# Pre-norm graph network, two layers, one Trainium2 core: second norm and adjacency products per row block, degree columns moved in front of the softmax, waits for one block instead of all

## The reference

```python
h = relu(layernorm(x))
feat = concat([h[src], h[dst]], axis=1)            # per edge; three kinds of edges, each with its W, b
e_f = relu(feat @ W_kind + b_kind)
logit = e_f @ W_a + b_a
alpha = segment_softmax(logit, dst)
z = segment_sum(alpha[:, None] * h[src], dst)
x = x + relu(concat([h, z]) @ W_hn_or_on + b)      # nodes 0..127: hn, the others: on
h = relu(layernorm(x))
# second layer: adjacency with self loops, deg = row sums, norm = deg^-0.5[row] * deg^-0.5[col]
x = x + segment_sum(norm[:, None] * (h @ W.T + b)[col], row)
```

## Time and profile before

| | us |
|---|---|
| median of 3 runs | 651.68 |
| runs | 649.97, 651.68, 654.79 |
| profiled execution, whole | 648.16 |
| its span in the profile | 646.0 |
| TensorE busy | 556.7 |
| VectorE busy | 453.9 |
| ScalarE busy | 306.2 |

### The profile page before, as it was taken

One profiled execution on the slowest core, in us unless ns is written; L12 is line 12 of the kernel. 1 busy time (PEld: TensorE's weight loads), 2 busy tenths in 40 slices (PEclk: granted clock), 3 DMA queues, 4 the chain that ended last, 5 costly groups with the idle time before them and its releaser, 6 DMA issues.

```text
span 646.0 us, 8205 instructions
## 1 busy us (share of the span) xinstructions
PE 556.7 (86%) x2376; PEld 409.7 (63%) x2377; DVE 453.9 (70%) x958; ACT 306.2 (47%) x485; POOL 173.4 (27%) x165
## 2 busy tenths in 40 slices
PE   0799999999879997979898997568949999779987
PEld 0688777776636765657575764324738788567865
DVE  6715256677986969999989786676795289783252
ACT  2613312114069996656655564499843182332200
POOL 2000300075364564566655553200030000000000
PEclk9999999999979999999998997888978899979999
DMA  8335453499999999999999999843355075130021
GB/s 326 124 132 172 145 192 136 144 243 380 324 331 343 296 328 339 316 330 349 341 342 303 332 317 339 224 145 111 106 225 198 16 245 185 61 102 29 0 82 49
DMA packets 55973, 140.51 MB, mean 218 GB/s; under 512 B 6274, under 2 KB 6402, under 8 KB 55938
## 3 DMA queue, kind: packets, MB, share of 16 engines
q0 software_dynamic: 20624, 74.98, 37.5%
q1 hardware_dynamic: 27072, 50.34, 22.7%
q10 hardware_dynamic: 8242, 14.75, 6.2%
HBM read 123.27 MB, written 16.78 MB: 217 GB/s over the span
## 4 chain that ended last, share of the span: by engine, by line
PE 51%; DVE 22%; DMA 11%; ACT 7%; issue 6%; POOL 2%; ACTq 1%; DVEq 0%; POOLq 0%
PE ps L638 30%; DMA gath<-tab_b,tabl_i 8%; PE ps L624 6%; PE ps L588 4%; ACT onehot L482 4%; DVE gath L893 4%; PE ps L797 3%; DVE gath L888 3%; PE ps L769 3%; DVE ring_l L868 2%; PE ps L782 2%; DVE onehot L910 2%; DMA gath<-tab_a,tabl_i 2%; ACT ring_h L435 1%; DVE logit_d L932 1%
## 5 line engine op out<-in xcount | busy, mean ns | idle before, releaser
L638 PE MATMUL ps<-ring_h,actT_h 128*128 128x512 f32 x520 | 225.8, 434 | 7.2 <-DVE actT_l L861 5.5
L638 PE MATMUL ps<-ring_h,actT_l 128*128 128x512 f32 x520 | 205.5, 395 | 0.0
L638 PE MATMUL ps<-ring_l,actT_h 128*128 128x512 f32 x520 | 204.9, 394 | 0.0
L482 ACT ACTIVATE onehot<-onehot,lgs 128x512 bf16<-128x512 bf16 x192 | 124.6, 712 | 72.3 <-DVE onehot L910 56.4
L435 ACT CAST ring_h<-raw 128x512 fp32r<-128x512 f32 x176 | 104.0, 616 | 105.9 <-PE ps L638 70.7
L868 DVE TENSOR_TENSOR ring_l<-raw,ring_h 128x512 fp32r<-128x512 f32 x176 | 116.9, 685 | 42.0 <-ACT ring_h L435 42.0
L638 PEld LDWEIGHTS ps<-ring_h,actT_h 128*128 128x128 f32 x520 | 99.6, 191 | 41.4 <-DVE actT_l L861 6.5
L588 PE MATMUL ps<-onehot 128*128 128x512 bf16 x292 | 84.1, 398 | 37.3 <-ACT onehot L482 34.2
L638 PEld LDWEIGHTS ps<-ring_h,actT_l 128*128 128x128 f32 x520 | 98.9, 190 | 22.2
L638 PEld LDWEIGHTS ps<-ring_l,actT_h 128*128 128x128 f32 x520 | 99.5, 191 | 20.1
L293 POOL DMA_INDIRECT gath<-tab_a,tabl_i x64 | 69.6, 1088 | 147.9 <-DVE gath L893 69.0
(11 more groups left out here) (162 smaller groups left out, 503.0 us busy)
## 6 DMA issues: line engine op xcount, KB each, us to landing
raw<-in_L_gnn_W_ho_dram SPq DMA_DIRECT2D x32, 256.0 KB
raw<-in_L_gnn_W_oo_dram SPq DMA_DIRECT2D x32, 256.0 KB
raw<-in_L_gnn_W_hh_dram SPq DMA_DIRECT2D x32, 256.0 KB
raw<-in_L_gnn_W_on_dram SPq DMA_DIRECT2D x32, 256.0 KB
...
```

Source lines behind the costliest of these rows:

```text
L482: ins = nc.scalar.mul(onehot[:, s, 1 + i, :], onehot[:, s, 1, :], lgs[:, i, q:q + 1])
L638: mm = nc.tensor.matmul(ps[:, first + m, :], w, v, start=(k == 0 and i == 0), stop=(k == KT - 1 and i == 2))
```

## The change

- **Buffers.** `adj` and the low parts of `hrow` move into `gath` and `topsum`, so that `adj` no longer waits for the stores from `stage`. The loads of `topsum` blocks 2 and 3 wait for the end of the z products.
- **Steps 13 to 15.** VectorE takes the last two tiles' edge rows at (13, 1) instead of (14, 0) and (14, 1), waits there for all edge rows and begins `adj` (`ADJ_AT`); the low parts of `hrow` follow (`ROWS_LOW_AT`); ScalarE rounds `hrow` at (13, 2). `copy_kind(2)` comes after chunk 15's `low_w` instead of at (15, 2).
- **Degrees.** TensorE's one-column matmuls stand at (14, 6) (bank 7) and before the last block's transposes (bank 4). VectorE waits for the first at (14, 7), ahead of `copy_kind(1)`. The inverse root is ScalarE's exp(-0.5 ln(deg)) with one Newton step.
- **Waits.** The z products wait for `attT` by block, the node products for `actT` by bank; the last chunk uses banks 4 to 7 and waits for no outputs.
- **Second norm.** Variance, root, norm, high and low part run by row block, between the updates; the adjacency products go block by block (`spread`).

```diff
-        hrow_h = sb("hrow_h", [P, NM, D], F32R, over="gath")
-        hrow_l = sb("hrow_l", [P, NM, D], F32R, over="gath", shift=4 * NM * D)
+        adj = sb("adj", [P, NM, N], F32, over="gath")
+        hrow_h = sb("hrow_h", [P, NM, D], F32R, over="gath", shift=4 * NM * D)
+        hl_gath = sb("hl_gath", [P, 2, D], F32R, over="gath", shift=8 * D)
+        hl_top = sb("hl_top", [P, 2, D], F32R, over="topsum", shift=8 * D)
+        hrow2_l = sb("hrow2_l", [P, NM, D], F32R, over="gath")
...
-        adj = sb("adj", [P, NM, N], F32, over="stage")
...
+        def hrow_l(m):
+            return hl_gath[:, m, :] if m < 2 else hl_top[:, m - 2, :]
...
-            for m in range(NM):
-                pool.dma_start(topsum[:, m, :], top_d[m * P:(m + 1) * P, :]).then_inc(s_topl[m], 16)
             pool.wait_ge(s_hr_l, NM)
             for m in range(NM):
                 pool.dma_start(hrow[:, m, :], x[m * P:(m + 1) * P, :]).then_inc(s_xr[m], 16)
+            for m in range(2):
+                pool.dma_start(topsum[:, m, :], top_d[m * P:(m + 1) * P, :]).then_inc(s_topl[m], 16)
+            pool.wait_ge(s_tp, TP_Z)
+            for m in range(2, NM):
+                pool.dma_start(topsum[:, m, :], top_d[m * P:(m + 1) * P, :]).then_inc(s_topl[m], 16)
...
+        EDGE_AT = {divmod(c * KT + k - EARLIER, KT): q for (c, k), q in SUM_AT.items() if q < ET - 2}
+        ADJ_AT = {(13, 1): ((0, 0), (0, 1)), (14, 0): ((1, 0),), (14, 1): ((1, 1),), (14, 2): ((2, 0),), (14, 3): ((2, 1),)}
+        ROWS_LOW_AT = {(14, 5): 0, (14, 7): 1, (15, 1): 2, (15, 2): 3}
...
+                    if (q, k) == (13, 2):
+                        act.wait_ge(s_edge, ET + GB)
+                        for m in range(NM):
+                            nc.scalar.copy(hrow_h[:, m, :], hrow[:, m, :]).then_inc(s_hr_h, 1)
...
-            act.wait_ge(s_edge, ET + GB)
-            for m in range(NM):
-                nc.scalar.copy(hrow_h[:, m, :], hrow[:, m, :]).then_inc(s_hr_h, 1)
+            act.wait_ge(s_degin, 1)
+            nc.scalar.activation(rs_root[:, :], rs_in[:, :], ACT.Ln).then_inc(s_dseed, 1)
+            act.wait_ge(s_dseed, 1)
+            nc.scalar.activation(rs_root[:, :], rs_root[:, :], ACT.Exp, scale=-0.5).then_inc(s_dseed, 1)
...
-                if k == 3:
-                    root(1)
...
-            for m in range(NM):
+            def row_root(m):
+                act.wait_ge(s_rsin, 2 + m)
+                nc.scalar.activation(rs_root[:, m:m + 1], rs_in[:, m:m + 1], ACT.Sqrt).then_inc(s_root, 1)
+            def row_high(m):
                 act.wait_ge(s_norm, NM + m + 1)
                 nc.scalar.activation(hrow_h[:, m, :], topsum[:, m, :], ACT.Relu).then_inc(s_hr_h, 1)
+            row_root(0)
+            row_high(0)
+            row_root(1)
+            row_high(1)
+            row_root(2)
+            rounds(q * KT, q * KT + 4)
+            row_high(2)
+            row_root(3)
+            rounds(q * KT + 4, (q + 1) * KT)
+            row_high(3)
...
             base = NM + NM * CH_EDGE
 
+            def adj_columns(bank, vector):
...
+                        mm = nc.tensor.matmul(ps[:, bank, m:m + 1], adj[:, k, m * P:(m + 1) * P], vector(k), start=(k == 0), stop=(k == NM - 1))
...
+                if c == 3:
+                    free = lambda m: pe.wait_ge(s_degin, 1)
+                def before(k):
+                    last_sums(q + c, k)
+                    if (c, k) == (2, 6):
+                        pe.wait_ge(s_adj, 1)
+                        pe.wait_ge(s_copied, base + 3)
+                        adj_columns(7, lambda k: ones[:, :])
+                chunk(q + c, NM, ms, free, before=before)
...
+                if m == NM - 1:
+                    pe.wait_ge(s_dinv, 1)
+                    pe.wait_ge(s_copied, base + 5)
+                    adj_columns(4, lambda k: dinv[:, k:k + 1])
...
-            pe.wait_ge(s_tl, TP_ATT)
             pe.wait_ge(s_hr_l, NM)
...
-                if f == 1:
+                if f == NM:
...
-                    for m in range(NM):
-                        for k in range(NM):
-                            mm = nc.tensor.matmul(ps[:, 6, m:m + 1], adj[:, k, m * P:(m + 1) * P], ones[:, :], start=(k == 0), stop=(k == NM - 1))
-                    mm.then_inc(s_deg, 1)
-                if f == 6:
-                    pe.wait_ge(s_dinv, 1)
-                    for m in range(NM):
-                        for k in range(NM):
-                            mm = nc.tensor.matmul(ps[:, 7, m:m + 1], adj[:, k, m * P:(m + 1) * P], dinv[:, k:k + 1], start=(k == 0), stop=(k == NM - 1))
-                    mm.then_inc(s_deg, 1)
-                if f == 7:
                     pe.wait_ge(s_dinv, 2)
                 c = slice(f * P, (f + 1) * P)
-                product(f, [p for k in range(NM) for p in passes(hrow_h[:, k, c], hrow_l[:, k, c], attT_h[:, k, :], attT_l[:, k, :])]
-                        ).then_inc(s_tp, 1)
-            pe.wait_ge(s_tl, TP_Z)
+                for k in range(NM):
...
+                        pe.wait_ge(s_tl, TP_H + k + 1)
+                    for i, (w, v) in enumerate(passes(hrow_h[:, k, c], hrow_l(k)[:, c], attT_h[:, k, :], attT_l[:, k, :])):
+                        mm = nc.tensor.matmul(ps[:, f, :], w, v, start=(k == 0 and i == 0), stop=(k == NM - 1 and i == 2))
+                mm.then_inc(s_tp, 1)
...
+            def z_ready(k):
+                pe.wait_ge(s_tl, TP_ATT + k + 1)
...
-                chunk(q + c, n * NM, ms)
+                chunk(q + c, n * NM, ms, before=z_ready if c == 0 else None)
...
-            pe.wait_ge(s_bsum, 8)
...
+            BANK_SUMMED = (1, 5, 5, 5, 2, 6, 7, 8)
...
+            def spread(k, f):
+                if k == 0:
+                    pe.wait_ge(s_bsum, BANK_SUMMED[f])
+                c = slice(f * P, (f + 1) * P)
+                for i, (w, v) in enumerate(passes(hrow_h[:, k, c], hrow2_l[:, k, c], adj_h[:, k, :], adj_l[:, k, :])):
+                    mm = nc.tensor.matmul(ps[:, f, :], w, v, start=(k == 0 and i == 0), stop=(k == NM - 1 and i == 2))
...
+            for k in range(2):
                 pe.wait_ge(s_hr_l, NM + k + 1)
-                for f in range(NM):
...
-                        ).then_inc(s_tp, 1)
-            pe.wait_ge(s_tl, TP_Z + KT)
-            chunk(q, 0, range(NM))
+                for f in range(KT - 1):
+                    spread(k, f)
+            for k in range(2):
+                spread(k, KT - 1)
+            pe.wait_ge(s_hr_l, NM + 3)
+            for f in range(KT):
+                spread(2, f)
+            pe.wait_ge(s_hr_l, NM + 4)
+            for f in range(KT):
+                spread(3, f).then_inc(s_tp, 1)
+            chunk(q, 0, range(NM), before=lambda k: pe.wait_ge(s_tl, TP_Z + max(k + 1, NM)))
...
-                pe.wait_ge(s_out, m + 1)
...
-                        mm = nc.tensor.matmul(ps[:, m, :], w, v, start=(k == 0 and i == 0), stop=(k == KT - 1 and i == 2))
+                        mm = nc.tensor.matmul(ps[:, NM + m, :], w, v, start=(k == 0 and i == 0), stop=(k == KT - 1 and i == 2))
...
+            def adj_part(stage_, half):
+                c = slice(2 * half, 2 * half + 2)
+                if stage_ < 2:
+                    step(nc.vector.tensor_tensor(adj[:, c, :], adj[:, c, :] if stage_ else count_d[:, 0, c, :], count_d[:, stage_ + 1, c, :], ALU.add))
+                else:
+                    for k in (2 * half, 2 * half + 1):
+                        ins = nc.vector.scalar_tensor_tensor(out=adj[:, k, :], in0=iota_f[:, :], scalar=rowid[:, k:k + 1],
+                                                             in1=adj[:, k, :], op0=ALU.is_equal, op1=ALU.add)
+                    if half:
+                        ins.then_inc(s_adj, 1)
+            def rows_low(m):
+                dve.wait_ge(s_hr_h, m + 1)
+                if m >= 2:
+                    dve.wait_ge(s_ohu, OS + ET + ET - 4)
+                nc.vector.tensor_tensor(hrow_l(m), hrow[:, m, :], f32(hrow_h[:, m, :]), ALU.subtract).then_inc(s_hr_l, 1)
...
-                    if (q, k) in ((13, 2), (15, 2)):
-                        copy_kind(q - 13)
+                    if (q, k) == (13, 2):
+                        copy_kind(0)
...
+                    if (q, k) == (13, 1):
+                        edge(ET - 2)
+                        edge(ET - 1)
+                        dve.wait_ge(s_edge, ET + GB)
+                    for part in ADJ_AT.get((q, k), ()):
+                        adj_part(*part)
+                    if (q, k) in ROWS_LOW_AT:
+                        rows_low(ROWS_LOW_AT[q, k])
...
                     if (q, k) == (14, 7):
+                        dve.wait_ge(s_deg, 1)
+                        nc.vector.tensor_copy(rs_in[:, :], ps[:, 7, 0:NM]).then_inc(s_degin, 1)
                         copy_kind(1)
...
+            copy_kind(2)
...
-            def rows_low(m):
-                dve.wait_ge(s_hr_h, m + 1)
```

(76 more changed lines are left out.)

64 lines of the change are left out of this document (17 added, 47 removed).

## The result

| | before | after |
|---|---|---|
| median, us | 650.83 (4 runs) | 643.03 (4 runs) |
| lowest to highest | 648.63 to 654.79 | 640.65 to 645.24 |
| profiled execution, whole | 648.16 | 643.92 |
| its span | 646.0 | 641.8 |

The ratio is 0.9888, with a 95% interval of 0.9845 to 0.9931: of 650.83 that is 7.3 us less (4.5 to 10.1), where 16.1 were forecast. The kernel became faster by about 1.1%, a little under half of what the prediction said.

The account below looks back on a forecast made before the run. TensorE, busy 86% of the span, was taken to bound the kernel through gaps and low-clock matmuls, with ScalarE's chain pacing 421 to 446. 8.6 paid, 11.8 and 12.9 saved: -16.1 us, 651.68 to 635.6, range 632 to 640.

Parts of the forecast that it names:

- (d): Front, chunk 15 to z products: chunk 15 moves by 8.6 plus 1.8 us; z starts 8.6 us later.
- The tail: After the z products: gaps shrink or go and adjacency products keep full clock, 12.9 us saved.
- The four gaps: TensorE after z: 1.37 us before node products, 8.24 before adjacency products, 1.36 after, 2.88 between last chunks; only 2.0 stays.
- The z stage: Start of z products to node products: degree runs leave, one cold start stays, 11.8 us saved.
- (a): Front, step (13, 1): VectorE waits for the last gather, then does adj parts; copy_kind(0) 4.2 us later.
- (b): Front, step (14, 7): VectorE waits for the degree columns; copy_kind(1) 4.3 us later, together 8.6.
- (c): Front, after copy_kind(1): VectorE has no idle time until the row maxima, which come 7.1 us later; table loads hidden.
- three signs: Wrong if copy_kind(0) near 417, VectorE's low rows over 2 us late for several blocks, or clock near 0.5 through chunk 15.
- the front: Steps 13 to 15 up to the start of the z products: 8.6 us paid.
- The front costs stack: Rival: several delays before the z products add about 10 us more, 645.6; chance 0.08.
- four terms: Chunk 14's VectorE work not absorbed (2 us), tables exposed (3), landing late (1), last transposes wait (4).
- TensorE stays at 1.2 GHz: Rival: after the columns, chunk 15 and z products run slow, 0.2 us a matmul, up to 665; chance 0.03.

Follow-up runs that it names:

- cols_early: Changed kernel with the second run of degree columns before block 1's transposes instead of block 3's: 632.43 us, ratio 0.9737 to the kernel before.
- tail_only: Kernel before with only the changed kernel's end (per-bank node waits, second norm by row block, last chunk on banks 4 to 7): 637.4 us, ratio 0.9795.
- fill: Changed kernel with 15 unused matmuls on zeros in TensorE's 3.33 us wait before block 1's transposes: 641.26 us, ratio 0.9834 to the kernel before.
- kind0_first: Changed kernel with kind 0 before the last two tiles' edge rows; adj parts, hrow rounding and low parts later: 637.25 us, ratio 0.9802 to the kernel before.
- wait_late: Changed kernel with VectorE taking kind 1 before its wait for the degree columns at (14, 7): 640.15 us, ratio 0.9806 to the kernel before.

## Why the prediction was wrong

The step that failed is the price of the second degree columns in (d): 3.47 us at full clock, with the transposes beside them at full clock too. They took 6.62 us at half clock, on the path. The smaller misses come first.

**The tail: right in mechanism, 1.9 us too much.** 12.9 us were forecast, 11.0 came. The wait before row 1 was 2.79 instead of 2.0. The node products' stretch, 523.90 to 568.97, is 45.07 us where the same 192 matmuls took 43.87 before; TensorE is idle 0.94 of it, waiting for ring parts. The four gaps went as forecast, and no third row was late. But "the clock no longer falls" was luck in part. The forecast left a wait of 2.0 us ahead of row 1 and gave the matmuls behind it the full clock. Behind waits of 2.79 and 2.77 us (changed kernel, cols_early) that held, and they took 17.3 us; behind 2.44, 2.97, 2.78 and 2.73 us (tail_only, fill, kind0_first, wait_late) the clock was 0.60, 0.50, 0.63 and 0.50 for the next 4 to 5 us, and they took 18.7, 19.9, 18.7 and 20.0. The term that is missing is 1.4 to 2.7 us, in four of six profiles.

**The z stage: right.** 12.1 for 11.8, one cold start, 23.54 for 23.8.

**(a), the wait for the last gather: right.** 4.9 for 4.2, and the landing read from the DMA share (417.1 against an issue at 408.96, 8.1 us) was 8.5 in the changed kernel. ScalarE's copies were hidden. kind0_first shows that the cost was real.

**(b), the columns in front of kind 1: right in size.** copy_kind(1) moved by 9.1, 4.2 of it here, for 4.3. That VectorE's wait rather than TensorE's own time carries it isn't shown, and wait_late's profile leans the other way (2.2 us at the end of chunk 15).

**(c): the row maxima** came 9.1 us late instead of 7.1, since TensorE's masks and sums ran at 1.2 GHz behind the columns (0.61 in 461.50 to 466.00) and VectorE waited for them at 471.92. It was not on the path: the last scaling waited for copy_top(3).

**(d), the failed step.** Chunk 15 ended 11.3 us late for 10.4, which is (a)'s excess and the clock as priced. But from there to the z products it took 14.3 us instead of 11.9, where the forecast had it 1.8 shorter: 4.2 us of error. The forecast's sum runs in steps from the end of chunk 15, at 480.1 (478.3 and 1.8; by its own rows 469.54 + 8.6 is 478.1, a slip of 0.2). It has the last transposes at 488.4, so the columns from 484.9. In us, from start to start:

| step | forecast | measured |
|---|---|---|
| end of chunk 15 to the second columns | 4.8 | 5.7 |
| the second columns | 3.5 | 6.7 |
| last transposes to the z products | 1.7 | 1.9 |

The columns are 3.2 of the error, and the eight transposes ahead of them, at 0.50 too, 0.65 (1.97 instead of 1.32); the other steps share the rest. So this miss is the clock. The row with 3.47 us was measured in the midst of dense z products, at 1.00 of the clock; in its new place TensorE had waited 3.33 us. fill shows that the wait is 2.0 of the 3.15 us (1.4 to 2.1 by the other profiles). The rest, 1.1 us, comes with a fall of the clock within the columns, which needs no wait.

The idle time that the columns were said to fill is no part of the error, though it was gone. By the forecast's own numbers copy_top(3) ends at 483.1 and the row sums at 483.8, so no gap was left between the scalings, and its sum adds the columns in full. What that overlooks is the other wait, the 3.3 us ahead of blocks 1 and 2, which the kernel before has as well. cols_early puts the columns there: 3.63 us at full clock, almost all in idle time, and 6.4 us less from the end of chunk 15 to the z products.

None of the three signs that the forecast named for being wrong was seen: copy_kind(0) started at 12.9 us from the gather, which is 421.9 in the times of before; one block alone was late, by 0.8 us more than forecast; and the clock was at 0.61 and 0.58 from 461.5 to 470 and at 1.00 for the rest of chunk 15. The step that failed had no sign.

**Sum.** 5.1 us in the front and 1.9 in the tail were missed, less 0.3 in the z stage: 6.7 of the 8.8 us between 16.1 and 7.3. The remaining 2 are within the interval; the clock behind the wait ahead of row 1, which stayed up in this profile and fell in others, may be part of them.

**The rivals.** "The front costs stack" (0.08) is the one that comes nearest, and for one of its four terms: the last transposes waited about 4 us longer, for the columns at half clock. The tables stayed hidden, the landing came 0.7 later than taken, and chunk 14 absorbed VectorE's extra work. "TensorE stays at 1.2 GHz" had the right mechanism and the right place. The clock came back within 9 us behind the first columns and within 5 behind the second, as the rows of before said. But the rival priced only the matmuls behind the columns and not the columns themselves. The Trainium skill (ScalarE: Activation LUTs, Table sets: the hidden batching unit) has log then exponential need one load, and its section What ACT_TABLE_LOAD costs adds a drain of 1.38 us to a load. The trace differs in both, and the measurement decides: two loads of 1.28 us again, and 0.24 us from the end of the first to the start of the second, 0.20 of it the logarithm, so that no drain shows.
